# A vision tower with a mixture of experts on one core: a new order for the last pair of groups, key patterns on another engine, slot scatters in pieces

## The reference

```
h = h + attn1(layernorm(h)) @ W_proj + b_proj
```

```
x2  = x + attn2(rms_norm(x) * norm1_w) @ w_out
m   = rms_norm(x2) * norm2_w
p   = softmax(m @ w_router); two largest experts of 16, weights normalised
moe = sum over the two of  weight * (silu(m @ gate_e) * (m @ up_e)) @ down_e
out = h + x2 + moe
```

## Time and profile before

| what | before |
|---|---|
| median of 3 runs | 309.94 us (308.75 to 310.29) |
| time of the profiled execution | 309.0 us |
| its span in the profile | 307.1 us |
| busy PE / DVE / ACT / POOL | 252.3 / 134.9 / 103.8 / 119.2 us |
| chain that ended last, share PE / DVE / POOL | 49% / 17% / 14% |
| granted TensorE clock, mean | 0.95 |

### The profile page before, as it was taken

One profiled execution on the slowest core, in us unless ns is written; L12 is line 12 of the kernel. 1 busy time (PEld: TensorE's weight loads), 2 busy tenths in 40 slices (PEclk: granted clock), 3 DMA queues, 4 the chain that ended last, 5 costly groups with the idle time before them and its releaser, 6 DMA issues.

```text
span 307.1 us, 5145 instructions
## 1 busy us (share of the span) xinstructions
PE 252.3 (82%) x1787; PEld 208.4 (68%) x1787; DVE 134.9 (44%) x347; ACT 103.8 (34%) x280; POOL 119.2 (39%) x130
## 2 busy tenths in 40 slices
PE   0999999889898897998999896504899999999910
PEld 0898788778597686887999686504566666667710
DVE  0063654767834587446567914640022222222114
ACT  0804942315713046424003611100444444444300
POOL 6033003295021693022890076173231555666220
PEclk9999999999999999999999997955999999999985
DMA  7503894005000040000000001692246442222026
GB/s 289 208 0 105 312 407 183 1 2 205 0 2 23 0 169 38 0 24 1 2 0 2 1 1 30 161 369 34 41 114 228 160 164 89 64 64 79 28 70 211
DMA packets 15661, 29.79 MB, mean 97 GB/s; under 512 B 6068, under 2 KB 10276, under 8 KB 15380
## 3 DMA queue, kind: packets, MB, share of 16 engines
q1 hardware_dynamic: 10948, 20.43, 19.5%
q10 hardware_dynamic: 2304, 5.16, 4.7%
q0 software_dynamic: 2384, 3.86, 4.1%
HBM read 25.36 MB, written 4.09 MB: 96 GB/s over the span
## 4 chain that ended last, share of the span: by engine, by line
PE 49%; DVE 17%; POOL 14%; issue 9%; DMA 5%; ACT 4%; POOLq 0%; ACTq 0%; SPq 0%; DVEq 0%
PE bank L1424 7%; PE bank L1307 5%; PE bank L1445 4%; PE bank L1421 4%; POOL slots L612 4%; PE bank L1171 4%; POOL experts L587 4%; PE bank L1181 4%; PE bank L1324 3%; PE bank L1370 3%; POOL rstd_a L529 2%; POOL parts L633 2%; DVE experts L870 2%; DMA front<-fw 2%; PE bank L1160 2%
## 5 line engine op out<-in xcount | busy, mean ns | idle before, releaser
L1171 PE MATMUL bank<-constants 128*128 128x96 f32 x246 | 33.1, 296 | 14.5 <-DMA slots<-slot_contents,slot_index 14.5
L1171 PEld LDWEIGHTS bank<-constants 128*128 128x128 f32 x246 | 32.1, 211 | 14.9 <-DMA slots<-slot_contents,slot_index 14.7
L1122 DVE TENSOR_TENSOR probs_by_key<-bank,probs_by_key 128x384 f32<-128x384 f32 x19 | 10.6, 557 | 55.2 <-PE bank L1424 48.5
L627 POOL DMA_INDIRECT front<-moe_in,probs_by_key x20 | 19.1, 957 | 34.5 <-DMA front<-moe_in,probs_by_key 30.5
L1307 PE MATMUL bank<-experts,front 96*96 96x208 f32 x160 | 29.3, 339 | 1.3 <-DVE experts L977 1.3
L1307 PEld LDWEIGHTS bank<-experts,front 96*96 96x96 f32 x160 | 25.9, 163 | 3.9 <-DVE experts L977 2.0
L587 POOL TENSOR_TENSOR experts<-experts 96x416 f32<-96x416 f32 x20 | 23.4, 1188 | 8.9 <-DVE experts L977 8.9
L977 DVE TENSOR_TENSOR experts<-bank,constants 96x416 f32<-96x416 f32 x40 | 21.3, 582 | 12.3 <-POOL experts L587 9.3
L612 POOL DMA_INDIRECT slots<-slot_contents,slot_index x16 | 15.8, 987 | 26.3 <-DVE slot_index L1082 22.2
L1424 PE MATMUL bank<-experts,probs_by_key 128*128 128x384 f32 x64 | 24.9, 512 | 0.0
L633 POOL DMA_INDIRECT parts<-front,probs_by_key x19 | 18.6, 980 | 13.8 <-DVE front L1126 9.8
(11 more groups left out here) (186 smaller groups left out, 478.2 us busy)
## 6 DMA issues: line engine op xcount, KB each, us to landing
experts<-wgu SPq DMA_DIRECT2D x6, 768.0 KB, 5.7
patches<-xp SPq DMA_DIRECT2D x6, 384.0 KB, 5.1
experts<-wdn SPq DMA_DIRECT2D x1, 2304.0 KB, 13.2
experts<-wgu ACTq DMA_DIRECT2D x4, 576.0 KB, 7.5
experts<-wgu SPq DMA_DIRECT2D x4, 576.0 KB, 4.2
front<-fw SPq DMA_DIRECT2D x1, 1840.0 KB, 7.2
experts<-wdn ACTq DMA_DIRECT2D x4, 288.0 KB, 5.7
experts<-wdn SPq DMA_DIRECT2D x4, 288.0 KB, 3.1
```

The lines of the kernel that those rows point to most:

```text
L627: pool.indirect_dma_start(xy[:, j * D:j * D + D], None, moe_in, bass.IndirectOffsetOnAxis(entry[:, j * 3 + 1:j * 3 + 2].bitcast(I32), 0)). ...
L1171: mm(bank[:, 0:96], eye, eye[:, 0:96], start=True, stop=True)
```

## The change

All engines take the first three pairs as before. The last pair is no longer emitted by `stages`: every engine's phases of groups 2 and 3 stand in an order written out by hand, in which the routing of the first half has its place.

- TensorE does `b5(2)` before `b4(3)`, splits `b6(2)` into its two tiles with `b5(3)` between them, and does `b8(2)` before `b7(3)`. Ahead of `b5(2)` stand 8 new warmers; the 15 of `b4(3)` go, and the 11 of `b7(3)` become 8.
- ScalarE does `b4(2)` before `b3(3)` and `b5(2)` before `b4(3)`. It writes the key patterns of groups 2 and 3 in a new function `keys`, as three activations with the scale taken from `group_of_row`; GpSimd leaves these two out.
- VectorE's `b3` is split: `weigh` is its second part. `b4(2)` stands before `weigh(3)`, `b5(2)` before `b4(3)`, and `place(0)` before `b5(3)`.
- GpSimd's 8 scatters of the first half come as 3 before `b6(2)`, 2 between `b6(2)` and `b6(3)`, and 3 behind. Before, 6 came ahead of `b6(2)` and 2 behind `b6(3)`.

```diff
-LEAD = (("A", 0), ("B", 0), ("B", 1), ("B", 2))
-FOLLOW = (("A", 1), ("A", 2), ("A", 3), ("B", 3))
+LEAD = (("A", 0), ("B", 0), ("B", 1))
+FOLLOW = (("A", 1), ("A", 2), ("A", 3))
...
-        def stages(a_phases, b_phases, routing):
+        def stages(a_phases, b_phases):
...
-                        if (what, group) == LEAD[-1] and n in routing:
-                            routing[n](0)
...
-                    if n == 0:
+                    if n == 0 and g < 2:
...
-            def scatter(q, ts):
+            def scatter(q, rows):
 
                 pool.wait_ge(filled, 16)
                 pool.wait_ge(fill_set, 4 + 2 * TOPK)
                 pool.wait_ge(gates_set, TOPK * (q + 1))
                 pool.wait_ge(idx_ready, q + 1)
-                for t in ts:
-                    for k in range(TOPK):
-                        pool.indirect_dma_start(slots, bass.IndirectOffsetOnAxis(sidx[:, k, t:t + 1], 0),
-                                                pay[:, k, t, :], None).then_inc(scattered, 16)
+                for n in rows:
+                    t, k = q * RT + n // TOPK, n % TOPK
+                    pool.indirect_dma_start(slots, bass.IndirectOffsetOnAxis(sidx[:, k, t:t + 1], 0),
+                                            pay[:, k, t, :], None).then_inc(scattered, 16)
 
             stages([a1, a2, a3, a4, nothing, a6, nothing, a8],
-                   [b1, b2, nothing, nothing, nothing, b6, nothing, nothing], {5: lambda q: scatter(q, range(3)), 7: lambda q: scatter(q, range(3, RT))})
+                   [b1, b2, nothing, nothing, nothing, b6, nothing, nothing])
+            for phase in (b1, b2):
+                phase(2)
+                phase(3)
+            scatter(0, range(3))
+            b6(2)
+            scatter(0, range(3, 5))
+            b6(3)
+            scatter(0, range(5, TOPK * RT))
             pool.wait_ge(pv2_done, 9)
             pool.memset(xT[:, 128:384], 0.0).then_inc(x_zeros, 1)
-            scatter(1, range(RT, TILES))
+            scatter(1, range(TOPK * RT))
...
-            stages([nothing, a2, a3, a4, a5, nothing, a7, nothing], [b1, b2, b3, b4, b5, b6, b7, nothing],
-                   {1: gate_exp, 2: copy_ranks})
+            def keys(g):
+
+                w = B[g]
+                act.wait_ge(rope_add, g * 5 + 1)
+                for n in range(G):
+                    last = act.activation(w.kbd2[:, :, :, n, :], w.kr, ACT.Identity,
+                                          scale=const("group_of_row", C)[:, n:n + 1])
+                last.then_inc(kbd2_ready, 1)
+
+            stages([nothing, a2, a3, a4, a5, nothing, a7, nothing], [b1, b2, b3, b4, b5, b6, b7, nothing])
+            b1(2)
+            gate_exp(0)
+            b1(3)
+            b2(2)
+            keys(2)
+            copy_ranks(0)
+            b2(3)
+            keys(3)
+            b3(2)
+            b4(2)
+            b3(3)
+            b5(2)
+            b4(3)
+            b5(3)
+            b6(2)
+            b6(3)
+            b7(2)
+            b7(3)
...
-                w = B[g]
-                softmax(g, 1, w, 104)
+                softmax(g, 1, B[g], 104)
+                weigh(g)
+
+            def weigh(g):
+                w = B[g]
                 row_sums(g, 1, w, 104)
...
-            stages([a1, nothing, a3, a4, a5, a6, nothing, a8], [nothing, b2, b3, b4, b5, b6, nothing, b8],
-                   {1: choose, 5: place})
+            stages([a1, nothing, a3, a4, a5, a6, nothing, a8], [nothing, b2, b3, b4, b5, b6, nothing, b8])
+            choose(0)
+            b2(2)
+            b2(3)
+            softmax(2, 1, B[2], 104)
+            weigh(2)
+            softmax(3, 1, B[3], 104)
+            b4(2)
+            weigh(3)
+            b5(2)
+            b4(3)
+            place(0)
+            b5(3)
+            b6(2)
+            b6(3)
+            b8(2)
+            b8(3)
...
-                    keep_busy(w.ps[3], (0, 14, 4, 15)[g])
+                    keep_busy(w.ps[3], (0, 14, 4, 0)[g])
...
-            def b6(g):
+            def b6(g, tiles=range(GT)):
                 w = B[g]
                 pe.wait_ge(ot2_a, g * 2 + 2)
                 pe.wait_ge(ot2_d, g + 1)
-                for t in range(GT):
+                for t in tiles:
...
-                keep_busy(w.ps[1], (7, 7, 0, 11)[g])
+                keep_busy(w.ps[1], (7, 7, 0, 8)[g])
...
-            stages([a1, a2, a3, a4, a5, a6, a7, a8], [b1, b2, b3, b4, b5, b6, b7, b8], {2: ranks})
+            stages([a1, a2, a3, a4, a5, a6, a7, a8], [b1, b2, b3, b4, b5, b6, b7, b8])
+            b1(2)
+            b1(3)
+            b2(2)
+            ranks(0)
+            b2(3)
+            b3(2)
+            b3(3)
+            b4(2)
+            keep_busy(B[2].ps[0], 8)
+            b5(2)
+            b4(3)
+            b6(2, range(1))
+            b5(3)
+            b6(2, range(1, GT))
+            b6(3)
+            b7(2)
+            b8(2)
+            b7(3)
+            b8(3)
             ranks(1)
```

## The result

The changed kernel takes 307.39 us at the median of 18 runs, the kernel before 309.14 on the same chip. The ratio is 0.9914, with a 95% interval of 0.9892 to 0.9937: faster by 0.9%, some 2.7 us. The forecast was 305.7, in a range of 304.5 to 308.4.

The account below looks back on a forecast made before the run. Scatters ahead of group 2's root were taken to bound the chain; the logits copy moves from 193.69 to 189.5, gaining 4.2 us. So 309.0 becomes 304.8, and with 0.94 to the median 305.7; range 304.5 to 308.4.

Parts of the forecast that it names:

- The bound: Last pair: six scatters on GpSimd hold group 2's root; in pieces it starts at 180.6 instead of 184.67, 4.07 us sooner.
- Key patterns at 0: Groups 2 and 3: patterns moved to ScalarE start b3(3) 0.6 us sooner, but nothing arrives at the end.
- The new order's times: Last pair up to b6: group 3's exponential 1.2 us later, b6(3) ends at 182.57 instead of 183.80, TensorE gains 1.2.
- Eight warmers at 0.117: TensorE's tail, b7(3): the eight warmers end at 187.27, 0.3 behind group 3's scaled rows, and set the end.
- the 2.22 us behind them: From the end of b7(3)'s warmers to group 3's logits copy: 2.22 us as before, giving 189.5.
- rival 1: TensorE's clock falls again in the wait between b7(2) and b8(2): time 306.8 to 308.0, chance 0.20.
- The tail behind the logits copy: From group 3's logits copy to the kernel's end: taken as unchanged; a longer tail would make the forecast wrong.
- The signs of being wrong: Last pair: root(2) past 182, b6(3) past 184, clock of 0.50 ahead of 189, or a longer tail behind the copy.
- Rival 3: Scatters beside VectorE's two-input scaled rows contend in full: root(3) 1.5 later, 1.2 lost, 306.9; chance 0.05.
- Rivals 2, 4 and 5: Last scatter lands later, 309.1 (0.08); clock falls earlier and stays, 313.7 (0.05); root(2) late for another reason, 309.9 (0.02).

Follow-up runs that it names:

- the trace in which the clock stayed: Changed kernel with 50 more warming matmuls on TensorE ahead of its wait for the scatters' landing: ratio 0.9925 to the kernel before, resting on two of six runs.
- without the covering ones: Kernel before with only GpSimd's scatters as 3, 2 and 3, and without b7(3)'s 11 warmers: 308.98 us, ratio 0.9974.
- pieces alone: Kernel before with only GpSimd's order of the last pair changed, scatters as 3, 2 and 3 around the roots: 305.24 us, ratio 0.9869.
- 15 warmers: Changed kernel, pieces of 3, 2 and 3 kept, with TensorE's tail as b7(2), 15 warmers, b7(3), b8(2), b8(3): 305.90 us, ratio 0.9879 to the kernel before.
- four ahead of the counts: Changed kernel with pieces 2, 2, 4, 12 warmers before b7(3), both b8 behind it, and 4 instead of 8 warmers before the second half's counts: 304.56 us, ratio 0.9860.
- the other version with these warmers: Changed kernel with pieces of 2, 2 and 4, 4 warmers before b8(2), 4 in b7(3), and 50 ahead of the landing: 309.79 us, ratio 1.0006.

## Why the prediction was right, and which term was too small

- **The bound** was named rightly. Scatters ahead of the root set group 2's end; put in pieces they alone give 0.9869, and in the changed kernel the root comes 3.9 us sooner where 4.07 was forecast. It still stands behind the third scatter, 1.3 us after its variance, not 0.7.
- **Key patterns at 0** is right: 1.0006 alone. The row that showed it was the second row maximum's wait for TensorE, not the 0.66 us wait for GpSimd, which goes and gives nothing.
- **The new order's times** were right to 0.3 us, the exponential's loss of 1.2 us behind ScalarE's copies included. The forecast gave the order no gain of its own at the end, but no price either. Without the pieces (but with the key patterns and the changed warmers) it costs 1.1%: a TensorE that is done sooner waits longer.
- **The step that was mis-sized** is "Eight warmers at 0.117" with the 2.22 us behind them: the tail at the high clock. In the profiled execution the logits copy is 2.26 us later than that; in the trace in which the clock stayed it is 0.3 later. This is rival 1, given 0.20, and its price of 1.1 to 2.3 us was right for its place. That the wait between b7(2) and b8(2) opens the way to it is what the runs with warmers in that wait and without the covering ones show. That the thin matmuls have a part in it, as the rival had it, is not shown: they were not tried by themselves, and in three traces (pieces alone, 15 warmers, four ahead of the counts) both b8 ran one behind the other with the clock at 1.00. With ten of the 18 executions at a mean clock of 0.940 or less, rival 1 should have had about half of the chance.
- **The tail behind the logits copy** was taken as unchanged. A low clock is paid there again, 1.3 us in the counts and their warmers; the forecast has no term for this.
- **The signs of being wrong** came in the profiled execution: a clock of 0.50 ahead of 189 and a longer tail. The time lies in the range because the range reached up to rival 1. It also lies nearer the forecast by luck: the base of 309.94 was the median of three runs, and that of 18 is 309.14; from there the same sum gives 304.9. By the ratio the gain is 2.7 us where 4.2 was forecast.
- **Rival 3**, contention of a scatter with VectorE's two-input rows: the pieces beside these rows took 1.04 us (181.61, 185.81 in the changed kernel's trace), as before. GPSIMD Engine Reference, Specifications, of the Trainium skill names that contention; here it is 0.08 us a piece and no more.
- **Rivals 2, 4 and 5** did not come: the last landing is as before (from the slot indices to the landing 12.4 us before, 12.5 now), the clock stood at 1.00 up to 185, and the root did move.

## What to carry to other kernels

When an engine is relieved and stands still, ask what its clock does next: matmuls that nothing waits for can be worth more than their own time, and the same matmuls placed behind the wait only cost. Take a change apart before it is kept; here one part of three carried it all and another without that one was a loss. Where a kernel's runs spread more after a change, look for what differs between its executions, here the clock, and don't judge by one profile.

## What had not been expected

- In the version with pieces of 2, 2 and 4 and both b8 behind b7(3), the clock fell while TensorE was recorded as busy nearly all the time (3.44 of 3.80 us, then 2.10 of 2.10). In the version with four warmers ahead of the counts it did not, with the same instructions up to there. Recorded busy time does not tell when the clock falls. TensorE: Matmul & The Clock Gate, What's actually happening, of the Trainium skill says that the low clock is the default and that activity releases it. The rows here agree that a standing TensorE comes down: the clock is at 0.50 through the wait for the landing in both kernels.
- With the 50 warmers ahead of the landing, the first list load took 3.46 us on the chain, in the same version without them 1.64. The same rise stands in the other version with these warmers (3.08). Why the load is slower there is open; no run was made for it.
- Which executions of one kernel fall to the low clock also stays open. Equal instructions gave both, in two pairs of traces: the changed kernel fell at about 185.7 and the version with 50 warmers, equal up to there, stayed at 1.00; of the two versions in the first point one fell and one did not.
